# Filling the whole buffer of sorted rows with padding rows at the start of a one-core language-model tower, in place of scattering padding rows behind each expert's rows

## The chip, the cores and the metric

The kernel runs on one core of one Trainium2 chip. The metric is the device time of one execution in microseconds (us). Before the change the median of three runs is 823.46 us (818.67 to 831.01). A profile of one further execution was taken; its times carry the argument.

## What is computed

2048 token ids (16 tiles of 128) go through a lookup, a linear attention with a running sum, a linear layer, a random-feature attention with a feed-forward part, and at the end a mixture of eight experts in which every token goes to one expert. Only the last part is touched by the change:

```python
def _L1_ffn_ref(hidden_states, router_w, expert_gate, expert_up, expert_down, shared_gate, shared_up, shared_down):
    x = hidden_states.reshape(-1, d)
    logits = jnp.einsum('td,ed->te', x, router_w)
    top_logit = jnp.max(logits, axis=-1)
    top_idx = jnp.argmax(logits, axis=-1)
    score = jax.nn.sigmoid(top_logit)
    onehot = jax.nn.one_hot(top_idx, n_experts, dtype=x.dtype)
    xs = x * score[:, None]
    g = jnp.einsum('td,edf->etf', xs, expert_gate)
    u = jnp.einsum('td,edf->etf', xs, expert_up)
    h = jax.nn.silu(g) * u
    eo = jnp.einsum('etf,efd->etd', h, expert_down)
    moe_out = jnp.einsum('te,etd->td', onehot, eo)
    sh = jax.nn.silu(x @ shared_gate) * (x @ shared_up) @ shared_down
    return (moe_out + sh).reshape(seq, bs, d)
```

## The kernel before, in words

Sizes: T = 16 tiles, E = 8 experts, P = 128, SPAN = 17, ROW = 513 floats (2052 bytes), 23 tiles of sorted rows.

**First stage: the tower.** Sixteen tiles go through a pipeline that is skewed by hand: `run_steps` (line 240) lets step u do stage "lag" of tile u - lag, in a fixed order on each engine. Each engine runs its instructions in order and waits on semaphores. Stage 4 of a tile is the router and the shared expert. There VectorE counts where each of the 128 tokens stands among its expert's rows (`c_slot`, line 874) and puts together `send`: the scaled input, the residual with the shared expert's result, and the token's number, 513 floats a token. GpSimd (POOL) scatters these 128 rows to the DRAM buffer `sorted_dram` with one indirect DMA a tile (`scat`, line 444, issue at line 449; semaphore `scattered`). `scat` stands last in POOL's order of a step (line 456), so the first one (t = 0) is the end of step u = 4. All of POOL's other stages, among them the inverse deviations that VectorE waits for (`r0` to `r6`, lines 375 to 407), stand in the same queue.

**The buffer.** `sorted_dram` (line 179) has for each expert a span of 17 * 128 rows, and one tile more at the end that holds padding rows alone. Expert e's rows start at row e * 17 * 128. An expert's last tile of 128 rows is rarely full, and what lies behind its rows must be padding rows: zeros, with a token number far out of range (`NOWHERE`), so that the store at the end leaves them out. `pads` (line 67) holds 128 such rows in SBUF, made by two fills on POOL (lines 344 and 354, semaphore `pads_ready`).

**Padding before the change.** SyncE (SP) stores `pads` to the extra tile once (line 275). Behind the last `scat`, POOL scatters `pads` eight times (lines 458 to 462), once for each expert, to the 128 rows from the end of that expert's rows (`pad_slots`, made by VectorE at line 943). SP waits for all of these (`scattered`, `pad_tile_stored`, `pads_stored`, lines 305 to 307) before it loads the first sorted tiles.

**SP's queue of transfers.** SP issues the weights in the order of need (lines 257 to 273), then the tile of padding rows (275), then experts 0 to 3 (line 281), and later experts 4 to 7 as their places in SBUF come free (lines 283 to 289). These are the transfers of one hardware queue, spread over 16 DMA engines. TensorE (PE) waits for the experts only ahead of the second stage (lines 1262 and 1263).

**Second stage: the experts.** VectorE works out a table of the 23 tiles (lines 945 to 973: the expert of each tile and its first row, semaphore `table_ready`). SP loads sorted tiles two at a time (line 296 for the input, line 300 for the residual), PE, ScalarE and VectorE compute the expert, POOL scatters the results to the output (line 469).

Of the kernel before, what the change touches and what calls it, by code (L numbers as in the profile page):

```python
# [8 lines left out]
ALU = mybir.AluOpType  # L9
# [5 lines left out]
U32 = mybir.dt.uint32  # L15
# [3 lines left out]
P = 128  # L19
# [12 lines left out]
def bass_lm_tower(nc, idx, table, w_qk0, w_v0, w_out0, cb, w_qk1, w_v1, w_out1, proj, w_ff1, w_ff2,  # L32
# [12 lines left out]
    E = w_router.shape[2]  # L45
# [4 lines left out]
    SPAN = T + 1  # L50
    ROW = 2 * D + 1
# [4 lines left out]
    with ExitStack() as ctx:  # L56
        def sb(name, shape, dt=F32):
            return ctx.enter_context(nc.sbuf_tensor(name, shape, dt))

        def sem(name):  # L60
            return ctx.enter_context(nc.semaphore(name))
# [5 lines left out]
        pads = sb("pads", [P, ROW])  # L67
# [35 lines left out]
        def columns(n):  # L103
            at[0] += n
            return cols_sb[:, at[0] - n:at[0]]
# [6 lines left out]
        partition = columns(1)  # L112
# [55 lines left out]
        base = sb("base", [P, E])  # L168
# [1 line left out]
        token = sb("token", [P, 1])  # L170
        slot = sb("slot", [P, 1])
        slot_u = sb("slot_u", [P, 1], U32)
        pad_slots = sb("pad_slots", [P, E], U32)
        rt = sb("rt", [P, 6 * E])
        flatS = S_sb[:].rearrange("p b a n -> p (b a n)")
        tile_expert = sb("tile_expert", [P, SORTED_TILES], I32)[:]
# [2 lines left out]
        sorted_dram = nc.dram_tensor("sorted_rows", [(E * SPAN + 1) * P, ROW], F32, kind="Internal").ap()  # L179
# [14 lines left out]
        preC_ready hC_ahead src5T_psum src5T_ready ffa_psum ffb_psum ffa_ready ffb_ready ff2_psum ff2_read  # L194
        src6_ready src6T_psum src6T_ready logit_psum logit_copied logit_read tanh_top onehot_ready count_psum counts_read
        slot_ready gate_psum up_psum tanh_gate gC_ready hT_ready sent_ready down_psum tile_done scattered
        pads_ready pads_known pads_stored pad_tile_stored table_ready
        xT_psum xT_ready eg_psum eu_psum tanh_eg eh_ready ehT_psum ehT_ready ey_psum ey_ready eg_ready
        table_step dve_step pool_step unused""".split()

# [1 line left out]
        S = {n: sem(n) for n in names}  # L202
# [44 lines left out]
        def tiles_of(i):  # L247

            of_round = [(s, i * MOE_SLOTS + s) for s in range(MOE_SLOTS)]
            return [(s, j) for s, j in of_round if j < SORTED_TILES] if isinstance(i, int) else of_round  # L250
# [4 lines left out]
        @block.sync  # L255
        def _(sp):
            sp.dma_start(idx_sb[:], idx).then_inc(S["idx_loaded"], 16)
            for dst, src in ((id_sb[:], ident), (cols_sb[:], cols)):
                sp.dma_start(dst, src).then_inc(S["small_loaded"], 16)
            for dst, src in ((qk0_sb, w_qk0), (v0_sb, w_v0)):  # L260
                sp.dma_start(dst, src).then_inc(S["qkv0_loaded"], 16)
            sp.wait_ge(gathered[0], 16)
            sp.dma_start(rows_sb[:], rows.partition_broadcast(P)).then_inc(S["vectors_loaded"], 16)
            sp.dma_start(causal_sb[:], causal).then_inc(S["out0_loaded"], 16)
            sp.dma_start(out0_sb, w_out0).then_inc(S["out0_loaded"], 16)
            sp.wait_ge(S["zero_ready"], 3)
            for h in range(8):
                sp.dma_start(proj_sb[DH * h:DH * h + DH, M * (h % 4):M * (h % 4) + M], proj).then_inc(S["proj_loaded"], 16)
            for dst, src in ((cb_sb, cb), (qk1_sb, w_qk1), (v1w_sb, w_v1), (hsum_sb[:], head_sum), (out1_sb, w_out1)):
                sp.dma_start(dst, src).then_inc(S["middle_loaded"], 16)  # L270
            for dst, src in ((ff1_sb, w_ff1), (ff2_sb, w_ff2), (router_sb[:], w_router), (sg_sb, w_shared_gate),
                             (su_sb, w_shared_up), (sd_sb, w_shared_down), (before_sb[:], before)):
                sp.dma_start(dst, src).then_inc(S["last_loaded"], 16)
            sp.wait_ge(S["pads_ready"], 2)
            sp.dma_start(sorted_dram[E * SPAN * P:, :], pads[:]).then_inc(S["pad_tile_stored"], 16)

            def load_experts(first, last, done):
                for e in range(first, last):
                    sp.dma_start(we[:, e * EXPERT:(e + 1) * EXPERT], w_experts[e]).then_inc(S[done], 16)

            load_experts(0, RESIDENT, "experts_loaded")

            sp.wait_ge(S["ffn0_psum"], T)
            sp.wait_ge(S["out1_psum"], T)
            load_experts(RESIDENT, freed_by_b, "late_loaded")
            sp.wait_ge(S["ff2_psum"], 2 * T)
            load_experts(freed_by_b, freed_by_ff, "late_loaded")
            sp.wait_ge(S["down_psum"], T)
            load_experts(freed_by_ff, E, "late_loaded")

            def first_row(j):
                return sp.value_load(tile_row[0:1, bass.ds(j, 1)], min_val=0, max_val=E * SPAN * P)

            def load(s, first):

                sp.dma_start(xm[s], sorted_dram[bass.ds(first, P), 0:D]).then_inc(x_loaded[s], 16)

            def load_home(s, first):

                sp.dma_start(home[s][:], sorted_dram[bass.ds(first, P), D:ROW]).then_inc(home_loaded[s], 16)  # L300

            sp.wait_ge(S["table_ready"], 1)
            sp.sem_inc(S["unused"], 1)
            first = [first_row(s) for s in range(MOE_SLOTS)]
            sp.wait_ge(S["scattered"], 16 * T)
            sp.wait_ge(S["pad_tile_stored"], 16)
            sp.wait_ge(S["pads_stored"], 16 * E)
            for s in range(MOE_SLOTS):
                load(s, first[s])
            for s in range(MOE_SLOTS):  # L310
                load_home(s, first[s])

            def load_next(i):

                for s, j in tiles_of(i):
                    sp.wait_ge(S["xT_psum"], j - (MOE_SLOTS - 1))
                    sp.sem_inc(S["unused"], 1)
                    load(s, first_row(j))

            def load_next_home(i):  # L320

                for s, j in tiles_of(i):
                    sp.wait_ge(home_stored[s], i * 16)
                    sp.sem_inc(S["unused"], 1)
                    load_home(s, first_row(j))

            load_next(1)
            with sp.Fori(2, ROUNDS - 1) as i:
                load_next(i)
                load_next_home(i - 1)  # L330
            load_next(ROUNDS - 1)
            load_next_home(ROUNDS - 2)
            load_next_home(ROUNDS - 1)
            for s in range(MOE_SLOTS):
                rounds = ROUNDS if s < len(tiles_of(ROUNDS - 1)) else ROUNDS - 1
                sp.wait_ge(home_stored[s], 16 * rounds)
# [3 lines left out]
        def _(pool):  # L340
# [102 lines left out]

            def scat(t):

                pool.wait_ge(S["slot_ready"], t * 2 + 2)
                pool.wait_ge(S["sent_ready"], t + 1)
                pool.wait_ge(S["tile_done"], t + 1)
                pool.indirect_dma_start(out=sorted_dram, in_=send[:], in_offset=None,
                                        out_offset=bass.IndirectOffsetOnAxis(ap=slot_u[:], axis=0)  # L450
                                        ).then_inc(S["scattered"], 16)

            run_steps([
                (3, hC), (0, r0), (3, r4), (2, kmx), (1, r1), (1, r2), (1, pA2), (2, pB), (3, pC), (3, r5), (1, r3),
                (3, r6), (0, pA), (4, scat),
            ])

            pool.wait_ge(S["pads_known"], 1)
            for e in range(E):
                pool.indirect_dma_start(out=sorted_dram, in_=pads[:], in_offset=None,  # L460
                                        out_offset=bass.IndirectOffsetOnAxis(ap=pad_slots[:, e:e + 1], axis=0)
                                        ).then_inc(S["pads_stored"], 16)

            tokens_out = out.rearrange("t p d -> (t p) d")
            def store(i):
# [148 lines left out]
        def _(dve):  # L614
# [311 lines left out]
            def then(ins):  # L926

                steps[0] += 1
                ins.then_inc(S["table_step"], 1)
                dve.wait_ge(S["table_step"], steps[0])  # L930
# [9 lines left out]
                return v.unsqueeze(1).broadcast_to([P, SORTED_TILES, E])  # L940

            tiles = number.unsqueeze(2).broadcast_to([P, SORTED_TILES, E])
            then(dve.tensor_tensor(pad_slots[:], base[:], partition.broadcast_to([P, E]), ALU.add))
            dve.sem_inc(S["pads_known"], 1)
            then(dve.tensor_tensor(count, base[:], start_row, ALU.subtract))

            then(dve.tensor_tensor(exceeds, count.unsqueeze(2).broadcast_to([P, E, T]),
# [418 lines left out]
```

## Time and profile before the change

| | us |
|---|---|
| median of 3 runs | 823.46 (818.67 to 831.01) |
| profiled execution | 832.05 |
| its span, first to last instruction | 830.2 |
| end of the first stage (last `send`) | 652.61 + 0.42 |
| first matmul of the second stage | 675.41 |

How to read it: the profile lists each engine's instructions with start and length from the span's start. A "chain" is the work that ended last, followed back from the last instruction, at each step to what released it. Views by window give the busy time of each engine in a stretch and what the DMA engines moved in it. PEclk is the granted clock of TensorE: 1.00 is 2.4 GHz and 0.50 is 1.2 GHz.

### The profile page before, as it was taken

Reading aid. Unit: us, or ns where it says so; the run is one execution under the profiler, and the core shown is the slowest. Engines: PE = TensorE matmul, PEld = TensorE weight load, DVE = VectorE, ACT = ScalarE, POOL = GpSimd, SP = SyncE. Lnnn points to the kernel's source line nnn. Section 1 sums busy time; section 2 is a strip of 40 time slices with the busy share of each in tenths; the row PEclk is TensorE's granted clock in tenths of the full one; section 3 lists DMA queues with packets and bytes.
Section 4 is the critical chain, followed back from the end, with each engine's and each line's share of the span. In section 5 each row is a group of like instructions: output and inputs, shape, how many; then the busy total and the mean of one; then the engine's idle time right before and its main releaser. Section 6 shows DMA issues by size and latency. Waiting matters only on the chain.

```text
span 830.2 us, 15028 instructions
## 1 busy us (share of the span) xinstructions
PE 716.4 (86%) x5674; PEld 582.1 (70%) x5675; DVE 494.2 (60%) x1218; ACT 243.1 (29%) x535; POOL 222.0 (27%) x401
## 2 busy tenths in 40 slices
PE   3588798989899998989899998988988339999995
PEld 2466687878787877878787877877777316556553
DVE  1466577876778777776768687876664402322331
ACT  1123333324242333334233333333231002212221
POOL 7313222232423232232423232231312301111111
PEclk9589899999999999999999999999899759999998
DMA  8930000000000000000000000000004731211210
GB/s 276 403 127 2 1 1 1 14 1 15 13 2 14 1 15 1 14 1 14 13 2 14 1 15 1 15 1 13 15 1 165 237 80 38 65 52 57 64 62 16
DMA packets 14910, 38.27 MB, mean 46 GB/s; under 512 B 3195, under 2 KB 9472, under 8 KB 13440
## 3 DMA queue, kind: packets, MB, share of 16 engines
q1 hardware_dynamic: 11056, 26.91, 9.2%
q0 software_dynamic: 3792, 10.51, 4.0%
q8 instruction: 42, 0.69, 0.3%
q14 instruction: 20, 0.16, 0.1%
HBM read 28.74 MB, written 9.58 MB: 46 GB/s over the span
## 4 chain that ended last, share of the span: by engine, by line
PE 57%; DVE 18%; issue 15%; POOL 6%; ACT 2%; DMA 2%; POOLq 0%; DVEq 0%; SPq 0%; ACTq 0%
PE ps L1000 52%; PE ps L1005 4%; DVE stats L628 3%; POOL rstd L378 3%; DVE yA L633 2%; POOL var_eps L377 2%; DVE mv L629 1%; DVE ctxbd L812 1%; DMA sorted_rows<-pads,pad_slots 1%; DVE H L644 1%; DVE qkA L681 1%; DVE hT L907 1%; DVE xA L669 1%; DVE tmpA L729 1%; POOL sorted_rows L460 1%
## 5 line engine op out<-in xcount | busy, mean ns | idle before, releaser
L1000 PE MATMUL ps<-yTC,we 128*128 128x128 f32 x1024 | 127.8, 282 | 0.9 <-ACT yTC L556 0.9
L1000 PEld LDWEIGHTS ps<-yTC,we 128*128 128x128 f32 x1024 | 121.6, 196 | 5.9 <-issue 4.6
L377 POOL TENSOR_TENSOR var_eps<-mv,ln_eps 128x1 f32<-128x1 f32 x112 | 26.8, 239 | 297.8 <-DVE mv L629 191.5
L1000 PE MATMUL ps<-we,yTA 128*128 128x256 f32 (+1 forms) x288 | 100.2, 480 | 2.9 <-ACT yTB L594 1.3
L1000 PE MATMUL ps<-we,yTB 128*128 128x256 f32 (+1 forms) x216 | 74.0, 473 | 0.0
L1000 PEld LDWEIGHTS ps<-we,yTA 128*128 128x128 f32 x288 | 54.3, 203 | 26.6 <-issue 21.1
L378 POOL TENSOR_TENSOR rstd<-var_eps,pow_half 128x1 f32<-128x1 f32 x112 | 64.5, 576 | 8.8
L1000 PE MATMUL ps<-we,ffT 128*128 128x256 f32 x256 | 63.9, 395 | 0.0
L1000 PEld LDWEIGHTS ps<-we,yTB 128*128 128x128 f32 x216 | 38.7, 191 | 22.9 <-issue 21.0
L1000 PEld LDWEIGHTS ps<-we,ffT 128*128 128x128 f32 x256 | 49.5, 199 | 6.4
L1000 PEld LDWEIGHTS ps<-voB,kf 128*128 128x128 f32 x256 | 38.6, 202 | 15.4 <-DVE kf L805 13.0
L1000 PE MATMUL ps<-voB,kf 128*128 128x64 f32 x256 | 38.3, 275 | 10.1 <-DVE kf L805 9.9
L469 POOL DMA_INDIRECT out<-tmpA,home x12 | 11.8, 985 | 130.1 <-DVE tmpA L989 130.1
L694 DVE TENSOR_TENSOR S_sb<-ps,causal_sb 128x512 f32<-128x512 f32 x64 | 40.9, 683 | 5.1 <-remote 4.6
L1000 PE MATMUL ps<-qfT,ctxbd 128*32 128x128 f32 x512 | 22.9, 336 | 17.2 <-DVE ctxbd L812 17.2
L1000 PE MATMUL ps<-yTA,we 128*128 128x128 f32 x256 | 34.5, 293 | 3.7 <-ACT yTA L485 1.9
L1000 PE MATMUL ps<-we,hT 128*128 128x256 f32 x128 | 36.0, 431 | 0.8 <-DVE hT L907 0.8
L1000 PEld LDWEIGHTS ps<-yTA,we 128*128 128x128 f32 x256 | 33.2, 209 | 4.7 <-issue 4.5
L1000 PE MATMUL ps<-proj_sb,qkB 64*128 64x256 f32 x256 | 36.3, 402 | 0.0
L644 DVE SCALAR_TENSOR_TENSOR H<-tmpA,rstd,preA 128x256 f32<-128x256 f32 x16 | 7.8, 485 | 47.8 <-POOL rstd L378 47.8
L980 DVE SCALAR_TENSOR_TENSOR kf<-kf,ps 128x512 f32<-128x512 f32 x12 | 8.3, 688 | 43.7 <-ACT kf L599 43.7
L1000 PEld LDWEIGHTS ps<-qfT,ctxbd 128*32 128x32 f32 x512 | 17.0, 131 | 23.2 <-DVE ctxbd L812 23.0
(187 smaller groups left out, 1360.9 us busy)
## 6 DMA issues: line engine op xcount, KB each, us to landing
we<-w_experts SPq DMA_DIRECT2D x8, 1536.0 KB, 23.2
home<-sorted_rows SPq DMA_DIRECT2D x23, 128.5 KB, 2.1
we<-w_ff SPq DMA_DIRECT2D x2, 1024.0 KB
rows_sb<-rows SPq DMA_DIRECT2D x1, 1664.0 KB
yA<-sorted_rows SPq DMA_DIRECT2D x12, 128.0 KB, 2.1
yB<-sorted_rows SPq DMA_DIRECT2D x11, 128.0 KB, 2.1
we<-w_qk SPq DMA_DIRECT2D x2, 512.0 KB, 3.6
we<-w_v SPq DMA_DIRECT2D x2, 256.0 KB, 3.9
```

Source lines behind the costliest of these rows:

```text
L377: link(pool.tensor_tensor(var_eps[:, k:k + 1], mv[:, k, 1:2], ln_eps[:], ALU.add))
L378: pool.tensor_tensor(rstd[:, k:k + 1], var_eps[:, k:k + 1], pow_half[:], ALU.pow).then_inc(S[f"rstd{k}_ready"], 1)
L460: pool.indirect_dma_start(out=sorted_dram, in_=pads[:], in_offset=None, out_offset=bass.IndirectOffsetOnAxis(ap=pad_slots[:, e:e + 1], axis=0)
L469: pool.indirect_dma_start(out=tokens_out, in_=ey[s], in_offset=None, out_offset=bass.IndirectOffsetOnAxis(ap=home[s][:, D:D + 1].bitcast(U ...
L628: link(dve.bn_stats(stats[:, k], src))
L629: dve.bn_aggr(mv[:, k], stats[:, k]).then_inc(S[f"var{k}_ready"], 1)
L633: return dve.tensor_scalar(dst, src, mv[:, k, 0:1], rstd[:, k:k + 1], ALU.subtract, ALU.mult)
L644: return dve.scalar_tensor_tensor(out=dst, in0=buf, scalar=rstd[:, k:k + 1], in1=rest, op0=ALU.mult, op1=ALU.add)
L669: dve.tensor_tensor(xA[:], by4(qk0), chunk_bias(qk0_bias, 4), ALU.add).then_inc(S["x_ready"], 1)
L694: dve.tensor_tensor(S_sb[:, b], by4(sc[b]), causal_sb[:].unsqueeze(1).broadcast_to([P, 4, P]), ALU.mult).then_inc(S["scores_masked"], 1)
L1000: return pe.matmul(o, a, b, start=start, stop=stop)
L1005: ins = pe.transpose(dst[:, c * P:(c + 1) * P], src[:, c * P:(c + 1) * P], id_sb[:])
```

## The change

SP fills the whole buffer with padding rows right after the weights: one transfer for each expert's span (17 tiles of 128 rows, the source read 17 times) and the one for the extra tile, which was there before. The first `scat` waits for all nine. POOL's eight scatters of padding rows, the instruction that made their row numbers and the two waits for them on SP are dropped.

```diff
@@ -272,7 +271,10 @@
             sp.wait_ge(S["pads_ready"], 2)
-            sp.dma_start(sorted_dram[E * SPAN * P:, :], pads[:]).then_inc(S["pad_tile_stored"], 16)
+            for e in range(E):
+                sp.dma_start(sorted_dram[e * SPAN * P:(e + 1) * SPAN * P, :].rearrange("(n p) r -> p n r", p=P),
+                             pads[:].unsqueeze(1).broadcast_to([P, SPAN, ROW])).then_inc(S["rows_cleared"], 16)
+            sp.dma_start(sorted_dram[E * SPAN * P:, :], pads[:]).then_inc(S["rows_cleared"], 16)
@@ -303,8 +305,6 @@
             sp.wait_ge(S["scattered"], 16 * T)
-            sp.wait_ge(S["pad_tile_stored"], 16)
-            sp.wait_ge(S["pads_stored"], 16 * E)
@@ -443,6 +443,8 @@
             def scat(t):
+                if t == 0:
+                    pool.wait_ge(S["rows_cleared"], 16 * (E + 1))
                 pool.wait_ge(S["slot_ready"], t * 2 + 2)
@@ -454,12 +456,6 @@
-            pool.wait_ge(S["pads_known"], 1)
-            for e in range(E):
-                pool.indirect_dma_start(out=sorted_dram, in_=pads[:], in_offset=None,
-                                        out_offset=bass.IndirectOffsetOnAxis(ap=pad_slots[:, e:e + 1], axis=0)
-                                        ).then_inc(S["pads_stored"], 16)
@@ -940,8 +936,6 @@
-            then(dve.tensor_tensor(pad_slots[:], base[:], partition.broadcast_to([P, E]), ALU.add))
-            dve.sem_inc(S["pads_known"], 1)
```

## Rows read from the trace of the kernel before

**Rows 1.** The page: busy shares, then DMA rate in 40 slices of 20.75 us.
```profile
PE 716.4 (86%) x5674; PEld 582.1 (70%) x5675; DVE 494.2 (60%) x1218; ACT 243.1 (29%) x535; POOL 222.0 (27%) x401
...
GB/s 276 403 127 2 1 1 1 14 1 15 13 2 14 1 15 1 14 1 14 13 2 14 1 15 1 15 1 13 15 1 165 237 80 38 65 52 57 64 62 16
```

**Rows 2.** Chain that ended last, from the last tile to the first expert: start, us, what.
```profile
652.61 0.43 DVE send L913
653.12 0.73 issue
653.85 0.96 POOL sorted_rows L449
654.81 0.30 issue
655.11 0.96 POOL sorted_rows L460
...
663.99 8.96 DMA sorted_rows<-pads,pad_slots
673.18 2.09 DMA yA<-sorted_rows
```

**Rows 3.** Waits of SP's queue, 640 to 700 us: total, times, longest.
```profile
SPq L307 <- DMA sorted_rows<-pads,pad_slots: 11.6, 1, 11.6
```

**Rows 4.** Timeline of VectorE: the operation dropped, the table's next and last.
```profile
652.95 0.16 DVE L943 TENSOR_TENSOR pad_slots<-base,cols_sb 128x8 uint32<-128x8 f32 x1
653.25 0.17 DVE L945 TENSOR_TENSOR rt<-base,cols_sb 128x8 f32<-128x8 f32 x1
...
659.54 0.18 DVE L973 TENSOR_TENSOR tile_row<-S_sb 128x23 int32<-128x23 f32 x1
```

**Rows 5.** Timeline of SP's queue: two loads, each with its table value fetched first.
```profile
676.87 0.33 SPq L296 DMA_DIRECT2D yA<-sorted_rows  x1
678.07 0.33 SPq L296 DMA_DIRECT2D yB<-sorted_rows  x1
```

**Rows 6.** Timeline of SP's queue: store of the padding tile, then the experts.
```profile
18.16 0.43 SPq L275 DMA_DIRECT2D sorted_rows<-pads  x1
18.63 3.27 SPq L279 DMA_DIRECT2D we<-w_experts  x2
```

**Rows 7.** DMA issues: KB each, median us from issue to landing.
```profile
sorted_rows<-pads SPq DMA_DIRECT2D x1, 256.5 KB, 16.6
```

**Rows 8.** Timeline of POOL at the first scatter and what stands behind it.
```profile
149.42 1.20 POOL L449 DMA_INDIRECT sorted_rows<-send,slot_u  x1 [1.67 <-DVE send L913]
150.65 0.74 POOL L442 TENSOR_TENSOR H<-H,rows_sb 128x256 f32<-128x256 f32 x1
151.34 0.20 POOL L377 TENSOR_TENSOR var_eps<-mv,ln_eps 128x1 f32<-128x1 f32 x1
151.62 0.57 POOL L378 TENSOR_TENSOR rstd<-var_eps,pow_half 128x1 f32<-128x1 f32 x1
```

**Rows 9.** Timeline of VectorE behind that: idle time and its releaser in brackets.
```profile
152.22 0.41 DVE L633 TENSOR_SCALAR yA<-H,mv,rstd 128x256 f32<-128x256 f32 x1 [0.80 <-POOL rstd L378]
```

**Rows 10.** Windows: busy us of each engine, PEclk, DMA share, GB/s; padding scatters.
```profile
658.50:660.50 2.00, 0.00 (x0) 0.00 (x0) 1.08 (x5) 0.00 (x0) 1.39 (x3) 0.50 0.96 386
660.50:662.50 2.00, 0.00 (x0) 0.00 (x0) 0.00 (x0) 0.00 (x0) 1.61 (x2) 0.50 1.11 238
...
664.50:666.50 2.00, 0.00 (x0) 0.00 (x0) 0.00 (x0) 0.00 (x0) 0.46 (x1) 0.50 1.02 144
...
660.50:669.50 9.00, 0.00 (x0) 0.00 (x0) 0.00 (x0) 0.00 (x0) 3.54 (x4) 0.50 1.03 185
```

**Rows 11.** DMA from 150 to 153 us in 40 slices: one scatter alone.
```profile
DMA  0000000000000006959799994000000000000000
GB/s 0 0 0 0 0 0 0 0 0 0 0 0 0 0 0 274 383 219 547 274 438 383 438 383 164 0 0 0 0 0 0 0 0 0 0 0 0 0 0 0
```

**Rows 12.** Timeline of PE: eight matmuls behind the idle time, and eight later.
```profile
677.84 6.04 PE L1000 MATMUL ps<-we,yTA 128*128 x8 [1.28 <-ACT yTB L594]
...
692.52 3.60 PE L1000 MATMUL ps<-we,yTA 128*128 x8
```

More of the change, by code:

```diff
@@ L172, in bass_lm_tower @@
         slot_u = sb("slot_u", [P, 1], U32)
-        pad_slots = sb("pad_slots", [P, E], U32)
         rt = sb("rt", [P, 6 * E])
@@ L196, in bass_lm_tower @@
         slot_ready gate_psum up_psum tanh_gate gC_ready hT_ready sent_ready down_psum tile_done scattered
-        pads_ready pads_known pads_stored pad_tile_stored table_ready
+        pads_ready rows_cleared table_ready
         xT_psum xT_ready eg_psum eu_psum tanh_eg eh_ready ehT_psum ehT_ready ey_psum ey_ready eg_ready
```

## The prediction, made before the changed kernel ran

> **What bounds the kernel now.** I read the page first: PE is busy 86% of the span, so most of the 830 us is matmul work that the change leaves alone, and the DMA engines, at up to 403 GB/s in the first 62 us, move almost nothing from there to 622 us [rows 1]. That empty stretch is what the change wants to use. Then the chain that ended last, at the seam of the two stages: from the last `send` at 652.6 it runs through the last scatter of tokens, eight scatters of padding rows on POOL and their landing to the first load of a sorted tile at 673.18 [rows 2]. The waits of SP's queue agree: 11.6 us at line 307, for the padding rows alone [rows 3]. So two places decide: the seam, where something is removed, and the first scatter at 149.42 [rows 8], where a wait is added. What lies between is unchanged.
>
> **What is removed at the seam.** Eight scatters, one each 1.27 us from 655.11 to 663.99 + 0.96, and 8 us until the last has landed [rows 2]; and one VectorE operation, which brings the table forward by 653.25 - 652.95 = 0.3 us [rows 4]. What is late next? The table: its last operation would end at 659.54 + 0.18 - 0.3 = 659.4 [rows 4]. Then SP fetches two first rows; in the steady loop two loads stand 1.2 us apart, of which 0.33 is the issue [rows 5], so a fetch is some 0.85 us and two are 1.7: first load at about 661.2. The last scatter of tokens, issued at 653.85, shares the engines with the last expert's 1.5 MB until about 659; alone its bytes move within 2 us of the issue's end [rows 2, 11]. I take 661.5 for the first load in place of 673.18: a gain of 11.7 us. Bounds: not over 673.18 - 659.4 = 13.8 us, and some 9 us if the last scatter or the last expert lands only at 664.
>
> **What is added: the bytes.** Eight spans of 17 * 128 rows of 2052 bytes are 35.72 MB, with the extra tile 35.98 MB. That is nearly as much as the whole execution moves now (38.27 MB). The padding tile, issued at 18.16, lands 16.6 us later at 34.8, because it queues behind the weights [rows 6, 7]; the new transfers take its place in the queue, so their bytes begin to move at about 33 us. The first scatter stands ready at 149.42 [rows 8]. Leaving 1 us for the last landing, no stall needs 35.98 MB in 115 us, that is 312 GB/s.
>
> **At what rate do padding rows go to DRAM?** No transfer of before writes megabytes through SP's queue; the nearest are the eight scatters at the seam, 2.1 MB of the same rows from the same tile. They show two rates. While the first 0.77 MB go (658.5 to 660.5) it is 386 GB/s. Then, with the engines' share still at 1.0, the next 9 us give 185 GB/s, single stretches 238 and 144 [rows 10]. Supply does not explain it: one scatter of 0.263 MB each 1.27 us is 207 GB/s, and the rate is below that also after POOL has stopped issuing at 665 (144). A lone scatter of tokens runs at the high rate and is over before the low one could show [rows 11]. So I read 386 as what a short burst gets and 185 as what writes of such rows sustain. The bounds are 144 and 386; I take 185, as the only figure over more than 2 us of pure writes. 35.98 / 0.185 = 194.5 us, less some 2 us for the burst at its start: the rows are cleared at 33 + 192.5 + 1 = 226 us, 77 us after 149.42.
>
> The Trainium skill, "DMA: Bandwidth & Descriptors", section "Latency and other measured facts", speaks against this change as well: copies between DRAM tensors whose partitions lie 512 KiB apart gave 207 GB/s, and at larger powers of two down to 103. Here a partition's successive rows lie 128 * 2052 bytes = 256.5 KiB apart, near such a power; by 207 GB/s, as an estimate, the rows would be cleared at 208 us, by 103 at 383 us. No run of before shows a stride of this kind.
>
> **What the wait holds up.** It stands in `scat(0)` on POOL. Behind it in POOL's queue stand the residual's addition and the inverse deviations of the next step, which before run at 150.65 and 151.34 with no idle time ahead of them [rows 8], and VectorE was already waiting 0.8 us for the result at 152.22 [rows 9]. POOL has no slack there, so VectorE stops within 3 us, and ScalarE and PE as soon as they have used what they have. All of the 77 us shows at the end, but for some 5 us of matmuls that PE can do ahead. Against these stands the clock: after the idle time at the seam eight matmuls took 6.04 us in place of 3.60 [rows 12]; a few such groups at 1.2 GHz after the stall cost about as much. I set both against each other.
>
> **Costs at nothing.** Experts 0 to 3 are queued behind the clearing and would land at about 245 us; PE wants them at 675. SP is held longer while it issues, but its next wait is for the last matmuls of the tower. The gathers of the embedding rows are issued by 25.5 us, ahead of the clearing.
>
> **Sum.** 832.05 - 11.7 + 77 = 897 us against the profiled execution. That execution is 8.6 us above the median of the runs shown, so on the scale of the median: 823.46 + 65.3 = 888.8, in round numbers 889 us (8% slower).
>
> **Rivals.**
> 1. *The writes keep the burst's rate.* 35.98 / 0.386 = 93 us, cleared at 127 us, before the first scatter asks: no stall, only the gain at the seam, 823.46 - 11.7 = 812 us. For it: 386 GB/s is a rate of the same rows [rows 10], a lone scatter holds it [rows 11], and SP's queue may write better than scattered rows. Against it: the rate fell within 2 us of writing. It decides from 312 GB/s up; at 283 GB/s stall and gain cancel. That is not slower than before, and at -1.4% within what can't be told from no change (some 2%, 16.5 us). The Trainium skill, same page, section "Measured (HBM→SBUF, 128 partitions, SWDGE, issued from GpSimd)", gives 425 GB/s for a transfer of 16 MB; by that, as an estimate, clearing takes 85 us and this rival holds. Those are reads, which the first 62 us here bear out (403) [rows 1], and not writes.
> 2. *The writes are slower still,* because 17 rows of a partition go 256.5 KiB apart while a scatter filled 256.5 KB in one piece. At 144 GB/s [rows 10] they take 250 us: cleared at 284, a stall of 135 us, 823.46 - 11.7 + 135 = 947 us; at half of 185 it would be above 1080.
> 3. *Partly hidden:* at 238 GB/s [rows 10], 151 us, cleared at 185, stall 36, 823.46 + 24 = 848 us. It belongs to the forecast's range.
> 4. *The seam does not give the time back,* since the last expert or the last tokens take the padding rows' place: 9 us of gain in place of 11.7, within the forecast.
>
> **How the numbers follow.** Forecast, rates of 160 to 250 GB/s: 0.58. Slower still: 0.10. The burst's rate or near it, no stall or a small one: 0.32, and in it 0.04 for over 2% faster, which needs 5 us more at the seam than I can find, so only by a seam and a run at their best. Faster 0.04, within 2% 0.28, slower 0.68. The forecast's own range goes from 238 to 144 GB/s: 848 to 947 us. The range over all reaches down to rival 1 with its scatter, 808, and up to 947.
>
> **What would show it.** Right: POOL idle ahead of the first scatter of tokens from about 149 to 226 us, released by DMA; an empty stretch of all engines; the DMA rate in the page's slices near 185 from 33 to 226; first load of a sorted tile some 8 us after the last `send`. Wrong: DMA quiet before 149 and the first scatter at its old place; or POOL waiting well beyond 284. If the stall is as long as said but the end is later by much less, the claim that POOL has no slack fails.

## The result, and the profile after the change

The changed kernel takes 924.26 us (median of 4 runs, 921.22 to 926.91) against 826.88 us for the kernel before on the same chip (818.67 to 831.01): a ratio of 1.121, interval 1.110 to 1.133, so 97 us slower by the medians. Ratios and intervals here and below are taken over comparable executions alone, so they differ by up to 0.004 from quotients of the medians. The profiled execution took 921.22 us, its span is 919.4 us.

The stall is where it was looked for. POOL's timeline (start, length, and in brackets the idle time ahead with its releaser) answers to [rows 8], VectorE's to [rows 9]:

```profile
147.94 0.73 POOL L417 TENSOR_TENSOR preA<-H,rows_sb 128x256 f32<-128x256 f32 x1
261.13 1.20 POOL L451 DMA_INDIRECT sorted_rows<-send,slot_u  x1 [112.46 <-DMA sorted_rows<-pads]
262.37 0.74 POOL L442 TENSOR_TENSOR H<-H,rows_sb 128x256 f32<-128x256 f32 x1
```
```profile
263.93 0.41 DVE L629 TENSOR_SCALAR yA<-H,mv,rstd 128x256 f32<-128x256 f32 x1 [111.58 <-POOL rstd L378]
```

Before, the first scatter went out at 149.42; now it waits 112.46 us for the padding rows, and the inverse deviation that stands two places behind it makes VectorE wait nearly as long. PE ran on to 159.5 with what it had (the matmuls that it did at this place before, too) and then stood for 105.61:

```profile
158.46 1.03 PE L994 MATMUL ps<-we,yTB 128*128 128x256 f32 x4
265.10 0.66 PE L999 MATMUL ps<-id_sb,yA 128*128 128x128 f32 x2 [105.61 <-DVE tmpB L826]
```

The rate at which the padding rows go out is read from windows of 25 us (busy time of PE, PEld, DVE, ACT and POOL, granted clock, DMA share, GB/s):

```profile
35.00:60.00 25.00, 19.77 (x175) 15.40 (x175) 18.42 (x40) 6.26 (x12) 4.94 (x11) 0.88 1.02 125
60.00:85.00 25.00, 19.36 (x202) 15.73 (x202) 15.85 (x35) 8.07 (x16) 6.96 (x14) 0.86 1.04 205
...
160.00:185.00 25.00, 0.00 (x0) 0.00 (x0) 0.00 (x0) 0.00 (x0) 0.00 (x0) 0.58 0.83 141
```

The rows begin to go out at about 33 us, as said: 339 GB/s from 33 to 34, with the end of the weights in it, and 101 from 34 to 35. 35.98 MB from there to 260.8 us are 158 GB/s on average, with the engines' share at 0.8 to 1.05 throughout. At the seam the chain now goes through the table, and the first load is at 763.88, 8.3 us after the last `send` begins, where [rows 2] has 20.6:

```profile
755.55 0.42 DVE send L909
...
762.04 0.19 DVE tile_row L967
...
763.88 2.14 DMA yA<-sorted_rows
```

So in the profiled pair: the first scatter is 111.7 us late, the last `send` 102.9 (755.55 - 652.61), the first load 90.7 (763.88 - 673.18), the end 89.2. The seam gives back 12.2 us. 8.8 us of the delay are made up between the first scatter and the last `send`. The granted clock goes with most of it, as two steps of the tower show, from the second scatter to the fourth, before and after:

```profile
187.00:262.00 75.00, 69.86 (x648) 61.02 (x647) 55.35 (x141) 25.74 (x58) 21.61 (x42) 0.95 0.02 8
```
```profile
297.00:369.00 72.00, 66.75 (x649) 58.65 (x648) 55.29 (x141) 25.64 (x58) 21.62 (x42) 1.00 0.03 9
```

The same number of matmuls takes 3.1 us less in the second, at a granted clock of 1.00 in place of 0.95. This is not shown to be an effect of the stall. From the first scatter of tokens to the sixteenth the profiled execution of before takes 504.4 us, the changed kernel 495.7, and two kernels below that never stall (tile by tile, and with rows of 2304 bytes) 498.6 and 498.4; the lines are before and tile by tile:

```profile
149.42:653.85 504.43, 461.60 (x4183) 403.18 (x4182) 359.06 (x929) 167.15 (x380) 140.54 (x271) 0.96 0.05 19
```
```profile
149.34:647.95 498.61, 454.40 (x4183) 396.72 (x4182) 359.14 (x929) 166.97 (x380) 140.23 (x270) 0.98 0.23 57
```

So some 6 of the 8.8 us are there without a stall: the profiled execution of before was a long one of its kind (832.05 us, median 826.88), with eight steps in a row at 0.95. By the medians the loss is 97 us, so about 3 us less than the wait of 112.5 and the seam's 12.2 leave.

### The profile page after: what moved, and what is told of

It reads as the page before. It is cut to its first block, busy times and chain, and to the rows that moved or that the text cites. A ratio compares the mean times of both kernels' runs of the same rounds, so it can differ in the third digit from the quotient of the medians.

```text
span 919.4 us, 15026 instructions
## 1 busy us (share of the span) xinstructions
PE 706.4 (77%) x5674; PEld 573.1 (62%) x5675; DVE 493.5 (54%) x1217; ACT 242.7 (26%) x535; POOL 214.5 (23%) x393
## 4 chain that ended last, share of the span: by engine, by line
PE 41%; SPq 23%; DVE 14%; issue 11%; DMA 6%; POOL 3%; ACT 2%; POOLq 0%; DVEq 0%
PE ps L994 38%; SPq L275 21%; DMA sorted_rows<-pads 5%; PE ps L999 2%; DVE stats L624 2%; POOL rstd L378 2%; DVE yA L629 1%; DVE ctxbd L808 1%; DVE mv L625 1%; POOL var_eps L377 1%; DVE qkA L677 1%; DVE hT L903 1%; DVE xA L665 1%; ACT qkA L600 1%; DVE H L640 1%
## 5 line engine op out<-in xcount | busy, mean ns | idle before, releaser
L999 PE MATMUL ps<-id_sb,yA 128*128 128x128 f32 x64 | 14.4, 310 | 127.4 <-DVE tmpB L826 105.6
L629 DVE TENSOR_SCALAR yA<-H,mv,rstd 128x256 f32<-128x256 f32 x32 | 19.4, 607 | 132.5 <-POOL rstd L378 131.2
L999 PEld LDWEIGHTS ps<-id_sb,yA 128*128 128x128 f32 x64 | 8.0, 151 | 131.3 <-DVE yA L629 121.1
L451 POOL DMA_INDIRECT sorted_rows<-send,slot_u x16 | 18.9, 1180 | 151.2 <-DMA sorted_rows<-pads 112.5
L501 ACT ACTIVATE rdenTA<-rdenA 128x256 f32<-128x256 f32 x16 | 6.7, 416 | 139.1 <-DVE rdenA L713 139.1
```

Of the source, the lines that this page charges most:

```text
L629: return dve.tensor_scalar(dst, src, mv[:, k, 0:1], rstd[:, k:k + 1], ALU.subtract, ALU.mult)
L999: ins = pe.transpose(dst[:, c * P:(c + 1) * P], src[:, c * P:(c + 1) * P], id_sb[:])
```

## The experiments

My theory after the result: the whole loss is one wait on POOL, and the wait is as long as it is because writes of these rows run at 158 GB/s. Open were whether the traffic by itself harms the tower, and why the rate is 158 and not the 386 of a burst.

**Take the wait away, keep the bytes.** The spans are cleared tile by tile, and each scatter waits only for the tiles that its rows can reach.

```diff
+        GROUPS = (0, 4, 9)
...
-            for e in range(E):
-                sp.dma_start(sorted_dram[e * SPAN * P:(e + 1) * SPAN * P, :].rearrange("(n p) r -> p n r", p=P),
-                             pads[:].unsqueeze(1).broadcast_to([P, SPAN, ROW])).then_inc(S["rows_cleared"], 16)
+            spans = sorted_dram[0:E * SPAN * P, :].rearrange("(e n p) r -> n p e r", n=SPAN, p=P)
+            for n in range(SPAN):
+                done = cleared[sum(n >= g for g in GROUPS[1:])]
+                sp.dma_start(spans[n], pads[:].unsqueeze(1).broadcast_to([P, E, ROW])).then_inc(done, 16)
...
-                if t == 0:
-                    pool.wait_ge(S["rows_cleared"], 16 * (E + 1))
+                if t in GROUPS:
+                    g = GROUPS.index(t)
+                    pool.wait_ge(cleared[g], 16 * ((GROUPS + (SPAN + 1,))[g + 1] - t))
```

> Edit: the same 35.98 MB are cleared at the same place of SP's queue, but tile n of all eight spans in one transfer, n from 0 to 16, in three groups with a semaphore each; scatter 0 waits for tiles 0 to 3, scatter 4 for 4 to 8, scatter 9 for the rest. My theory (the whole loss is one wait of 112 us on POOL, for writes that run at some 160 GB/s): tiles 0 to 3 are 8.4 MB, done at about 85 us, ahead of the first scatter at 149; the others are done at about 150 and 260, ahead of scatter 4 (about 299) and scatter 9 (about 487). No stall; what is left is the seam's gain of 11.7 us, so 11 to 12 us below the kernel before, about 815 us. Rival (the traffic itself slows the tower, by instruction fetches or weights behind the writes): a loss stays although POOL never waits for the clearing, 830 us or more.

Measured: 816.7 us against 828.95, ratio 0.985 (0.978 to 0.992): 12 us below the kernel before, as the theory said. The bytes are under way until about 225 us, earlier than the 260 expected, and the tower does not feel them:

```profile
149.34 1.20 POOL L455 DMA_INDIRECT sorted_rows<-send,slot_u  x1 [1.68 <-DVE send L913]
```
```profile
110.00:135.00 25.00, 24.83 (x233) 21.43 (x231) 17.71 (x42) 9.94 (x23) 5.82 (x13) 1.00 1.03 196
...
185.00:210.00 25.00, 23.84 (x228) 20.83 (x227) 16.82 (x40) 9.11 (x21) 7.01 (x13) 1.00 1.04 193
```

The first scatter is at its old place, PE is as busy as without the traffic (24.83 us from 110 to 135 in the kernel before as well), and the seam's gain is whole (first load 8.3 us after the last `send`). The rows go at 191 to 206 GB/s here, a little faster than in the changed kernel's order, but again at half of 386.

**The stride.** Only the order of the rows in DRAM changes.

```diff
-                sp.dma_start(sorted_dram[e * SPAN * P:(e + 1) * SPAN * P, :].rearrange("(n p) r -> p n r", p=P),
+                sp.dma_start(sorted_dram[e * SPAN * P:(e + 1) * SPAN * P, :].rearrange("(p n) r -> p n r", p=P),
```

> Edit: the spans are walked so that the 17 rows of a partition lie next to each other in DRAM (steps of 2052 bytes) instead of 256.5 KiB apart; bytes, number of rows and queue are the same. Theory A (what writes of 2052-byte rows sustain, whatever their order): 150 to 185 GB/s as in the changed kernel, cleared at 230 to 260 us, 890 to 925 us. Rival B (the stride near a power of two is what halves the rate): the rate goes to 300 GB/s or more, the stall goes or is under 10 us, 815 to 825 us.

Measured: 930.65 us, one run; the first scatter at 268.3 us. Both are a little beyond what Theory A allowed, and far from Rival B. The stride is not the cause:

```profile
60.00:85.00 25.00, 19.60 (x201) 15.89 (x200) 17.84 (x38) 8.11 (x13) 6.96 (x14) 0.86 1.05 184
...
210.00:235.00 25.00, 0.00 (x0) 0.00 (x0) 0.00 (x0) 0.00 (x0) 0.00 (x0) 0.50 1.03 148
```

**The rows' length.** 576 floats a row; loads and `send` keep to the first 513.

```diff
-    ROW = 2 * D + 1
+    ROW = 2 * D + 64
...
-                sp.dma_start(home[s][:], sorted_dram[bass.ds(first, P), D:ROW]).then_inc(home_loaded[s], 16)
+                sp.dma_start(home[s][:], sorted_dram[bass.ds(first, P), D:2 * D + 1]).then_inc(home_loaded[s], 16)
...
```

> Edit: a row of the buffer is 576 floats (2304 bytes, a multiple of 256) instead of 513, and whole rows are written, so that no two rows share a line of memory; 40.4 MB are cleared instead of 35.98. Theory A1 (DRAM takes so many bytes a second): 158 GB/s again, 256 us, cleared at about 290 us, 30 us later than in the changed kernel, about 950 us. Rival C (rows that begin and end inside a line cost extra reads): the rate goes to 300 GB/s or more, cleared at 165 us or before, 815 to 835 us.

Measured: 815.42 us, one run. With 12% more bytes the rate is 381 to 411 GB/s from 35 to 135 us, more than double the average of 158, and the first scatter goes out at 151.00 without waiting for the clearing:

```profile
60.00:85.00 25.00, 18.67 (x205) 15.44 (x206) 18.06 (x39) 8.40 (x14) 6.97 (x14) 0.93 1.04 404
```

What of a row's length matters had to be taken apart. First, fewer and longer pieces, with the rows still 2052 bytes:

```diff
...
+            sp.wait_ge(S["wide_ready"], 2)
-                sp.dma_start(sorted_dram[e * SPAN * P:(e + 1) * SPAN * P, :].rearrange("(n p) r -> p n r", p=P),
-                             pads[:].unsqueeze(1).broadcast_to([P, SPAN, ROW])).then_inc(S["rows_cleared"], 16)
+                sp.dma_start(sorted_dram[e * SPAN * P:(e + 1) * SPAN * P, :].rearrange("(p n) r -> p (n r)", p=P),
+                             we[:, 0:SPAN * ROW]).then_inc(S["rows_cleared"], 16)
+            sp.wait_ge(S["rows_cleared"], 16 * (E + 1))
             load_experts(0, RESIDENT, "experts_loaded")
...
+            dve.memset(wide[:, :, 0:2 * D], 0.0).then_inc(S["wide_ready"], 1)
+            dve.memset(wide[:, :, 2 * D:ROW].bitcast(U32), NOWHERE).then_inc(S["wide_ready"], 1)
```

> Edit: the source is 17 padding rows side by side in the place of the experts' weights, so that each partition writes one piece of 34,884 bytes; the bytes and the queue are the same, the experts are loaded after the clearing. VectorE fills the source first, some 10 us at the start. Theory A (bytes to DRAM): about 160 GB/s, cleared at about 260 us, 920 us. Rival D (the number of rows, 2176 a transfer, is what costs): 300 GB/s or more, no stall or one under 10 us, 815 to 830 us.

Measured: 829.85 us, one run. The rate is 422 to 434 GB/s and there is no stall:

```profile
60.00:85.00 25.00, 20.78 (x180) 17.25 (x180) 18.74 (x39) 7.62 (x15) 6.56 (x13) 0.86 0.99 422
```

What keeps it from 815 is for the most part the fill: VectorE is busy 502.2 us in place of 493.5, at the start, where the tower waits for it (first scatter at 160.10, about 10 us late). So DRAM takes more than 400 GB/s of writes for some 85 us on end. The bytes do not cost, nor does the stride; and the number of rows does not, since the kernel with rows of 2304 bytes wrote as many. What is left is something at the joints between rows.

**The joints.** Three kernels tell the cases apart. The first has rows of 2112 bytes (`ROW = 2 * D + 16`, otherwise as above):

> Edit: the buffer's rows are 528 floats (2112 bytes, 33 times 64) and whole rows are written; 37.0 MB are cleared. With 2304 bytes (9 times 256) the rate was 380 to 411 GB/s. Theory: it is the line of memory that counts, and 64 bytes is a line; then the rate is above 312 GB/s, no stall, about 815 us. Rival: a piece must start at a multiple of 256 bytes; then the rate stays near 160 to 200 GB/s, cleared at 220 to 265 us, 880 to 930 us.

The second writes 2052 bytes at a pitch of 2304 (otherwise the kernel with rows of 2304 bytes):

```diff
-                sp.dma_start(sorted_dram[e * SPAN * P:(e + 1) * SPAN * P, :].rearrange("(n p) r -> p n r", p=P),
-                             pads[:].unsqueeze(1).broadcast_to([P, SPAN, ROW])).then_inc(S["rows_cleared"], 16)
+                sp.dma_start(sorted_dram[e * SPAN * P:(e + 1) * SPAN * P, 0:2 * D + 1].rearrange("(n p) r -> p n r", p=P),
+                             pads[:, 0:2 * D + 1].unsqueeze(1).broadcast_to([P, SPAN, 2 * D + 1])).then_inc(S["rows_cleared"], 16)
```

> Edit: rows lie 2304 bytes apart as in the third experiment, but the clearing writes only the first 2052 bytes of each; the last 252 bytes of each row are left as they were (nothing reads them). Bytes 35.98 MB as in the changed kernel. Theory E (a piece that begins or ends inside a line costs, once for each such end): one such end a row in place of two, so 220 to 300 GB/s, cleared at 155 to 200 us, a stall of 5 to 50 us, 820 to 865 us. Rival F (two rows that share a line get in each other's way): no line is shared, so above 350 GB/s, no stall, about 815 us. Rival G (one such end is as bad as two): 160 to 200 GB/s, 880 to 925 us.

The third is the second with all of a row's contents one float further on (`1:2 * D + 2` in the transfer, and so in the loads and in `send`):

> Edit: the sixth experiment (rows 2304 bytes apart, 2052 bytes of each written) with everything in a row moved on by 4 bytes, so that each piece begins 4 bytes behind a multiple of 256; the number of bytes and of pieces is the same and no two rows share a line of 64 bytes. Theory H (it is a piece's unaligned start that costs): 150 to 210 GB/s, cleared at 205 to 275 us, a stall of 55 to 125 us, 870 to 930 us. Rival F (it is the line shared by two rows that costs): 375 GB/s as in the sixth experiment, no stall, about 813 us.

Measured, one run each: 807.43, 813.84 and 812.81 us, no stall in any (first scatters at 150.06, 148.41 and 151.18). The window from 60 to 85 us of the three, in this order:

```profile
60.00:85.00 25.00, 22.31 (x208) 18.89 (x209) 16.87 (x38) 8.40 (x14) 6.95 (x14) 0.80 1.06 386
```
```profile
60.00:85.00 25.00, 21.49 (x223) 17.43 (x223) 18.18 (x41) 9.03 (x18) 6.96 (x14) 0.93 1.06 374
```
```profile
60.00:85.00 25.00, 19.50 (x199) 16.02 (x197) 15.35 (x33) 7.76 (x14) 6.94 (x14) 0.86 1.06 375
```

Per row the three take the same time, about 5.5 ns (2112 bytes at 386 GB/s, 2052 at 374 and at 375). So a piece that ends inside a block of memory costs nothing that shows (the second), nor does one that begins 4 bytes into a block and ends inside one (the third). What is left is the block that two neighbouring rows share. How large is it?

> Edit: rows of 2080 bytes (65 times 32), whole rows written: every second row begins in the middle of a 64-byte line, and every such line is shared by two rows. 36.5 MB. If 32 bytes is alignment enough: 386 GB/s as with 2112 bytes, no stall, about 810 us. If 64 bytes is what counts: under 280 GB/s, cleared after 164 us, 15 us of stall or more, 830 us or above.

Measured: 812.89 us, one run, the first scatter at 152.12 behind VectorE alone, and 380 GB/s:

```profile
60.00:85.00 25.00, 21.53 (x207) 18.06 (x207) 15.85 (x36) 7.76 (x14) 6.96 (x14) 0.81 1.06 380
```

Rows of 2080 bytes share blocks of 64 bytes, but none of 32 (counted from a buffer that begins on such a block). At 2052 bytes neighbours share one of 32 at seven joints of eight, one of 16 at three of four, one of 8 at every second, and none of 4. So the loss of rate goes with two rows in one block, and the block is of 32 bytes or less; which size between 8 and 32 it is was not tried. One rival is left open: in packed rows of 2052 bytes the pieces begin at every multiple of 4 inside a block, and only a start 4 bytes in was tried on rows that share nothing.

**The seam before.** My 185 GB/s came from the padding rows scattered at the end of the kernel before. The same cause should show there.

> Edit: the kernel before, with its eight scatters of padding rows at the end, but with rows of 2304 bytes. Theory (the 185 GB/s at the seam, from which the prediction took its rate, is the price of rows that end inside a line, and not of scattering as such): the rate at the seam follows POOL's issue, about 230 GB/s, the last padding rows land 2 to 3 us after the last issue in place of 8 us, the first sorted tile is loaded some 5 us earlier. Rival (scatters go at that rate whatever the rows): the landing still takes about 8 us. Time: 5 us less than before by the first, equal by the second, both within the scatter of single runs; the seam in the trace decides.

Measured: 818.19 us, one run, against a median of 825.8. In the chain the landing takes 2.80 us in place of 8.96 [rows 2], SP's wait is 4.7 us in place of 11.6 [rows 3], and the first load comes 14.4 us after the last `send` (645.19 and 659.60) in place of 20.6:

```profile
656.57 2.80 DMA sorted_rows<-pads,pad_slots
```
```profile
SPq L307 <- DMA sorted_rows<-pads,pad_slots: 4.7, 1, 4.7
```

**Timed versions.** Three of these kernels were timed in rounds: the changed one with rows of 2304 and of 2112 bytes, and the kernel before with rows of 2112.

> The third experiment's kernel again (the changed kernel with rows of 2304 bytes, whole rows written), timed in three rounds. Theory: no stall, and the seam's 11.7 us are kept, so 0.980 to 0.990 of the time before, about 815 us. Rival (the 12% more bytes in loads and scatters of rows cost something): 0.990 to 1.0.

> The fifth experiment's kernel (the changed kernel with rows of 2112 bytes) timed in three rounds, as the version that may be best. No stall and fewer bytes than with 2304: 0.975 to 0.990 of the time before. If the seam's gain is all there is: 0.986; if the kernel before loses more than that at the seam or to the clock: 0.980 or under.

> Edit: the kernel before, scatters of padding rows at the end included, with rows of 2112 bytes. In the seventh experiment (2304 bytes) the wait for the padding rows at the seam fell from 11.6 to 4.7 us. Theory: 7 us less than before, 0.990 to 0.993; the whole clearing with unshared lines would then be worth only the 4.7 us that are left. Rival (a part of the clearing's gain is the clock or scatter of runs): 0.995 to 1.0.

| kernel | us | before, same chip | ratio, interval |
|---|---|---|---|
| the change, rows of 2304 bytes | 809.96 | 825.8 | 0.980 (0.973 to 0.987) |
| the change, tile by tile, rows of 2052 | 816.7 | 828.95 | 0.985 (0.978 to 0.992) |
| the change, rows of 2112 bytes | 815.52 | 823.76 | 0.991 (0.988 to 0.994) |
| before, rows of 2112 bytes | 820.21 | 825.34 | 0.996 (0.992 to 1.000) |

The first three are 1 to 2% faster than the kernel before, and none is shown to be more than 2% faster. Which of them is best these runs cannot say, since each was compared on a chip of its own: the kernel with rows of 2112 bytes ran in 807.43 us once on one chip and in 815.52 here, with 0.991 just outside the 0.975 to 0.990 expected. The last row shows what the clearing is worth once rows share no block. SP waits 5.2 us there for the padding rows, and the first load comes 14.3 us after the last `send`; with the clearing it is 8.3, so some 6 us are left to win. The gain of this version is 5 us by the medians and 0.996 by the ratio. That is less than the 7 us expected (0.990 to 0.993) and in the range of the rival, though its seam is 6.2 us shorter than before. So clearing 36 MB early is a small gain at best, and the large loss comes of the single wait together with the rows' length.

## Why the prediction was right, and where it was off

The direction, the mechanism and the place were right; the size was not (65 us forecast, 97 measured, 924 inside the range of 808 to 947).

- *The stall.* "Cleared at 226 us, 77 us after 149.42": the wait was there, 112.46 us long, until 260.8. The term that was mis-sized is the rate, 185 forecast and 158 measured: above the 144 that ended the forecast's range, but just below the rates of 160 to 250 to which its chance was given. That 185 is what such rows sustain at the seam held. The 386 was not a rate of 0.77 MB of padding rows: 0.11 MB in that window are the last expert's, and among the 0.66 MB of POOL's queue are the 0.26 of the last tokens, since next to nothing of that queue had moved before 658.5. The 2 us taken off for a burst did not show in the clearing either (101 GB/s from 34 to 35 us). What I missed is that "such rows" was the point: it is the row's length, and the seventh experiment removes the low rate at the seam as well.
- *No slack on POOL.* Right: VectorE waited 111.58 us behind it. PE went on for about 9 us after POOL stopped, and where it took up work again it was 106.7 us late (265.10 in place of 158.40), 5 us less than the scatter, as forecast; but the next scatter (297.43 in place of 187.01) was 110.4 late, so little of this was kept. I had set work ahead against a low clock after the stall and put nothing. In the profiled pair 8.8 us came back over the tower, but two kernels without a stall show some 6 of them, so nothing is near the mark.
- *The seam.* 11.7 us forecast, 12.2 measured; the table is what comes last there now, as said. From its end to the first load SP took 1.65 us (763.88 - 762.23), where 1.7 was worked out and some slack added.
- *Costs at nothing.* The experts behind the clearing cost nothing: at the seam the chain goes through the table and not through them. The tile-by-tile kernel shows no cost of 36 MB of writes beside the tower either (498.6 us from the first scatter to the last, 504.4 before).
- *Rivals.* The first (the burst's rate) was false for these rows and true for rows of 2080, 2112 and 2304 bytes; its 812 us is near what those kernels run at (807 to 816). The second had the sign of the error right, and its cause wrong: with rows laid together the rate was no better. The Trainium skill ("DMA: Bandwidth & Descriptors", "Latency and other measured facts") has copies slow when the pitch from partition to partition is 512 KiB or a larger power of two. In the changed kernel that pitch is 2052 bytes, and the 256.5 KiB are the step from row to row within a partition, so the estimates of 208 and 383 us did not carry over, and it is chance that 260.8 lies between them. No run here shows a loss by such a step: 260 KiB, the step with rows of 2080 bytes, ran at 380 GB/s. The Trainium skill has 425 GB/s for a read of 16 MB ("DMA: Bandwidth & Descriptors", "Measured (HBM→SBUF, 128 partitions, SWDGE, issued from GpSimd)"); writes met it here once the pieces were long, with 422 to 434.

## What to carry to other kernels

When a wait is placed in an engine's queue, what counts is everything behind it: one early wait for the whole buffer made the kernel 97 us slower, the same bytes with a wait for only the tiles in reach cost nothing that shows. Take the rate of a long transfer from the longest stretch of the same rows, not from a burst, and ask what is special about those rows. Give rows in DRAM a length that is a multiple of 32 bytes, so that neighbours written by different pieces do not share a block; 2080, 2112 and 2304 bytes were tried here.

## What the runs showed of the hardware that was not expected

Writes of 2052-byte rows to neighbouring places ran at 125 to 206 GB/s (windows of 25 us) in three orders, and at 374 to 411 GB/s when no two rows shared a block of 32 bytes, whether the pieces began on such a block or 4 bytes behind it. Why the shared block costs so much is not settled here, nor why the changed kernel's rate was 141 to 165 GB/s from 160 to 235 us, while the tower stood still, and 170 to 205 from 60 to 160, while it ran. With pieces of 34,884 bytes, where a joint comes once in 17 rows, no loss showed. A short transfer does not reveal it: at the seam 0.66 MB of scattered rows went out within 2 us before the rate fell [rows 10], and a lone scatter of 0.26 MB is over before that [rows 11].
